# Two graph layers on one core: 36 batches of 31 sorted and 14 plain tiles, edge rows loaded whole in two parts, layer 1's half packed by ScalarE

## The reference

```
h  = max(layernorm(x), 0)                                   # layer 0, GIN
m  = relu(h[src] + e16 @ W_edge.T + b_edge)                 # per edge
a  = h + segment_sum(m, dst)                                # per node
x  = x + relu(batchnorm(a @ W1.T + b1)) @ W2.T + b2
h  = max(layernorm(x), 0)                                   # layer 1
y  = relu(concat(h[src], e64) @ M_W.T + M_b)                # per edge
x  = x + relu(concat(h, segment_sum(y, dst)) @ U_W.T + U_b)
```

## Time and profile before

| what | value |
|---|---|
| timed runs, median of 3 | 4224.73 us |
| profiled execution: span from first to last instruction | 2879.7 us |
| its own time beside the span | none given by the profile; the timed median less the span is 1345.0 us |
| PE busy | 2027.5 us, 70% of the span |
| POOL busy | 2097.2 us, 73% |
| DVE busy | 1529.9 us, 53% |
| ACT busy | 958.6 us, 33% |
| mean granted TensorE clock | 0.824 |
| HBM read, written | 296.20 MB, 268.18 MB |

### The profile page before, as it was taken

How to read it: one execution, slowest core, us unless ns; L and a number is a source line. 1 busy time by engine, 2 the same in 40 slices (tenths; PEclk the granted TensorE clock), 3 DMA queues, 4 the chain that set the end, 5 groups by cost and what they waited for, 6 DMA issues and landing times.

```text
span 2879.7 us, 74534 instructions
## 1 busy us (share of the span) xinstructions
PE 2027.5 (70%) x25733; PEld 1830.1 (64%) x25733; DVE 1529.9 (53%) x2605; ACT 958.6 (33%) x2153; POOL 2097.2 (73%) x2185
## 2 busy tenths in 40 slices
PE   4678777677775777767676676766768776778772
PEld 4567666666665766657565576656647666667662
DVE  6655445344443445444454444534568776777671
ACT  2433333333332333323333233333353332323230
POOL 5777777777777777777777777777537777777774
PEclk9987887878878888788888888887869888888885
DMA  8877766777668766677667776675639998989861
GB/s 269 237 194 214 219 198 174 195 219 207 196 174 207 227 194 190 183 212 224 191 182 190 219 210 197 175 198 133 150 110 266 233 211 215 220 213 225 208 160 46
DMA packets 707917, 567.80 MB, mean 197 GB/s; under 512 B 495308, under 2 KB 609216, under 8 KB 703224
## 3 DMA queue, kind: packets, MB, share of 16 engines
q1 hardware_dynamic: 628632, 403.50, 55.1%
q0 software_dynamic: 69440, 107.94, 12.5%
q10 hardware_dynamic: 9632, 53.14, 5.3%
HBM read 296.20 MB, written 268.18 MB: 196 GB/s over the span
## 4 chain that ended last, share of the span: by engine, by line
POOL 30%; PE 24%; DMA 16%; issue 14%; SPq 7%; DVE 5%; ACT 3%; POOLq 1%; DVEq 0%; ACTq 0%
POOL edge_store L753 15%; POOL gathered_rows L783 15%; PE ps_w L1228 10%; DMA src_store<-arena 8%; PE ps_p L1163 6%; SPq L564 5%; PE ps_r L1216 4%; DMA side<-attr 4%; DMA edge_store<-side,slot_idx 2%; ACT arena L926 1%; DMA gathered_rows<-node_table_l,plain_slot 1%; PE ps_b L1198 1%; SPq L491 1%; DMA arena<-edge_store 1%; DVE ranking L1524 1%
## 5 line engine op out<-in xcount | busy, mean ns | idle before, releaser
L783 POOL DMA_INDIRECT gathered_rows<-node_table_l,plain_slot x1116 | 1066.1, 955 | 359.3 <-issue 327.2
L753 POOL DMA_INDIRECT edge_store<-side,slot_idx x1054 | 1023.3, 971 | 344.8 <-issue 325.0
L1228 PE MATMUL ps_w<-arena 128*64 128x128 f32 (+1 forms) x9040 | 922.0, 293 | 204.5 <-ACT window L934 195.7
L1228 PEld LDWEIGHTS ps_w<-arena 128*64 128x64 f32 x9040 | 787.0, 158 | 264.7 <-ACT window L934 147.3
L939 ACT ACTIVATE arena<-arena 128x512 f32<-128x512 f32 (+1 forms) x616 | 366.3, 595 | 1533.1 <-PE ps_w L1228 925.9
L1163 PE MATMUL ps_p<-w_both,side 80*128 80x128 f32 x3228 | 519.6, 317 | 425.2 <-DMA side<-attr 344.1
L1163 PEld LDWEIGHTS ps_p<-w_both,side 80*128 80x128 f32 x3228 | 461.5, 223 | 446.4 <-issue 404.0
L1630 DVE TENSOR_TENSOR arena<-ps_c,dst_rel 128x1024 f32<-128x1024 f32 (+1 forms) x476 | 525.9, 1105 | 336.1 <-PE ps_w L1228 332.7
L1615 DVE TENSOR_SCALAR arena<-arena,iota_p 125x512 bf16<-125x512 bf16 (+1 forms) x442 | 155.9, 370 | 604.5 <-DMA src_store<-arena 371.6
L1216 PE MATMUL ps_r<-tab,arena 125*128 125x64 bf16 x5100 | 245.9, 202 | 102.5 <-DVE arena L1615 60.8
L1639 DVE TENSOR_TENSOR arena<-ps_r,arena 128x512 f32<-128x512 f32 (+1 forms) x476 | 297.6, 625 | 20.3 <-PE ps_r L1216 13.4
(11 more groups left out here) (124 smaller groups left out, 1057.4 us busy)
## 6 DMA issues: line engine op xcount, KB each, us to landing
edge_store<-zeros SPq DMA_DIRECT2D x34, 3300.0 KB
arena<-edge_store SPq DMA_DIRECT2D x34, 1650.0 KB, 10.7
src_store<-arena SPq DMA_DIRECT2D x204, 256.0 KB
side<-attr SPq DMA_DIRECT2D x172, 256.0 KB
arena<-edge_store SPq DMA_DIRECT2D x34, 1056.0 KB
arena<-edge_store SPq DMA_DIRECT2D x34, 594.0 KB
plain_store<-plain_e SPq DMA_DIRECT2D x35, 512.0 KB
side<-plain_store SPq DMA_DIRECT2D x35, 512.0 KB
```

The lines of the kernel that those rows point to most:

```text
L753: pool.indirect_dma_start(out=store, in_=stage[:, c, i, :], in_offset=None, out_offset=bass.IndirectOffsetOnAxis(ap=slot_idx[:, s, t + i:t ...
L783: pool.indirect_dma_start(out=rows[s][:, i, :], out_offset=None, in_=table[layer], in_offset=bass.IndirectOffsetOnAxis(ap=plain_slot[:, s, ...
L1228: mm = pe.matmul(ps_sum[layer][t % 2][:, 0:width], msg[:, slot, t, :], dst_match[:, slot, t, 0:width], start=(first and t <= layer), stop= ...
```

## The change

Batches become 31 sorted and 14 plain tiles, 36 of them (1620 tiles of room for 1612 used); groups and plain parts are equal in number, and the last plain part has 6 tiles. All loops end after 36 groups; one `last_plain` is left in each layer. The two plain units have 8 and 6 tiles.

In layer 0 a group's rows are loaded whole (528 bytes each, so that a partition's columns are one run): columns 0 to 23 (units 0 to 2) to a double buffer `early`, columns 24 to 49 (units 3 to 6) to a single buffer `late_rows`, which is loaded for the next group when the last unit of this group has been used and packed. ACT reads the marks of each part separately. After each relu of a sorted unit ACT copies the 66 floats with the marks and layer 1's half of each row to one of two slots of `halved` (`pack`) and stores them to a new table `edge_half` (`store_half`), whose rows are in the order of the reader. Layer 1 loads its part from there, in runs of 8448 and 4752 bytes a partition. `load_early` of group m+2 waits for unit 2 of group m used and packed. The core of the diff:

```diff
-PLAIN = 16
+PLAIN = 14
-TILES = 1645
-BATCHES = TILES // BATCH
-NB = BATCHES - 1
-PARTS = BATCHES
+NB = 36
+TILES = NB * BATCH
+BATCHES = NB
+PARTS = NB
+EARLY_UNITS = 3
+EARLY = EARLY_UNITS * UNIT
+LATE = NODE_COLS - EARLY
-PAIR_HALVES = (-1, 0, 1, 1, 2, 2, 3, 4)
+PAIR_HALVES = (-1, 0, 1, 1, 2, 3, 4)
-PAIR_UNITS = (0, 0, 1, 2, 3, 4, 5, 6)
+PAIR_UNITS = (0, 0, 1, 2, 3, 4, 5)
...
+    edge_half = nc.dram_tensor("edge_half", (NB, P, NODE_COLS * HALF_ROW), F32, kind="Internal").ap()
...
-            def load_edges(g, p):
-                sp.dma_start(edge[p], store_groups[bass.ds(g, 1), 0:CAP * NODE_COLS, 0:HALF_ROW]
-                             .rearrange("a (p j) c -> p (a j) c", j=NODE_COLS)).then_inc(dense_sems[0].e_landed[p], 16)
+            def load_early(g, p):
+                sp.dma_start(early[p].rearrange("p j c -> p (j c)"), store_groups[bass.ds(g, 1), 0:CAP * NODE_COLS, :]
+                             .rearrange("a (p j) c -> p (a j c)", j=NODE_COLS)[:, 0:early_cols]).then_inc(dense_sems[0].e_landed[p], 16)
+
+            def load_late(g):
+                sp.wait_ge(dense_sems[0].rows_used, units(g - 1, NU - 1) + 2)
+                sp.wait_ge(halves_packed, units(g - 1, NU - 1))
+                sp.dma_start(late_rows.rearrange("p j c -> p (j c)"), store_groups[bass.ds(g, 1), 0:CAP * NODE_COLS, :]
+                             .rearrange("a (p j) c -> p (a j c)", j=NODE_COLS)[:, early_cols:]).then_inc(dense_sems[0].late_landed, 16)
             def load_edges_part(g, p, k):
                 j, nj = LOAD_PARTS[k]
-                sp.dma_start(edge[p][:, j:j + nj, :], store_groups[bass.ds(g, 1), 0:CAP * NODE_COLS, D:D + HALF_ROW]
-                             .rearrange("a (p j) c -> p (a j) c", j=NODE_COLS)[:, j:j + nj, :]).then_inc(dense_sems[1].e_landed[p], 16)
+                sp.dma_start(edge[p][:, j:j + nj, :].rearrange("p j c -> p (j c)"),
+                             edge_half[bass.ds(g, 1), :, j * HALF_ROW:(j + nj) * HALF_ROW].rearrange("a p c -> (a p) c"))\
+                    .then_inc(dense_sems[1].e_landed[p], 16)
...
             def next_edges(m, s):
                 group_landed(m + 2)
-                sp.wait_ge(dense_sems[0].rows_used, units(m, NU - 1) + 2)
-                load_edges(m + 2, s)
+                sp.wait_ge(dense_sems[0].rows_used, units(m, EARLY_UNITS - 1) + 2)
+                sp.wait_ge(halves_packed, units(m, EARLY_UNITS - 1))
+                load_early(m + 2, s)
...
+                if not (isinstance(m, int) and m + 2 >= NB):
+                    load_late(m + 2)
                 for q in range(2):
                     load(m + 1, q if not isinstance(m, int) or m + 1 <= LAST_PREPARED else NQ + q)
                 store_plain(m)
...
+            def pack(g, gn, p, u):
+                slot, nt = (p + u) % 2, UNITS[u][1]
+                if not (isinstance(gn, int) and src_stores(gn, p, u) == 0):
+                    act.wait_ge(halves_stored[slot], src_stores(gn, p, u) * 16)
+                act.activation(halved[:, slot, 0:nt, :], edge_rows(p, u)[:, :, META:META + HALF_ROW], ACT.Copy).then_inc(halves_packed, 1)
+
+            def store_half(g, p, u):
+                slot, (j, nt) = (p + u) % 2, UNITS[u]
+                act.wait_ge(halves_packed, units(g, u))
+                act.dma_start(edge_half[bass.ds(g, 1), :, j * HALF_ROW:(j + nt) * HALF_ROW].rearrange("a p c -> (a p) c"),
+                              halved[:, slot, 0:nt, :].rearrange("p t c -> p (t c)")).then_inc(halves_stored[slot], 16)
...
                 for u, (j, nt) in enumerate(UNITS):
                     if layer == 0:
+                        if u == 1:
+                            read_late(m + 1, p)
                         for i in range(2 * u + 2, min(2 * u + 4, NH)):
                             copy_spread(m + 1, p, i)
                     act.wait_ge(d.rows_used, units(m + 1, u) + 2)
                     relu(layer, at + u, (par + u) % 2, nt)
+                    if layer == 0:
+                        pack(m + 1, n + s, p, u)
+                        if u:
+                            store_half(m + 1, p, u - 1)
...
+                if layer == 0:
+                    store_half(m + 1, p, NU - 1)
```

More of the change, by code:

```diff
@@ L220, in attr_loads, with metas @@
     return m * (NL // 2) + (FIRST_LOADS // 2 + q // 2 + 1)
+def metas(layer, g, k):
+    return g * 4 + 2 * (k + 1) if layer == 0 else g + 1
 def src_stores(bn, p, u):
@@ L420, in build @@
         src_matched = sem("src_matched")
+        halves_packed = sem("halves_packed")
+        halves_stored = [sem(f"halves_stored{s}") for s in range(2)]
         src_stored = [sem(f"src_stored{s}") for s in range(2)]
@@ L664, in turn @@
                         load(m, (2, 3, 4, 5).index(u) + 2)
-                    if u == 4:
+                    if u == 4 and not (isinstance(m, int) and m + 2 >= PARTS):
                         next_plain_idx(0, n, s)
@@ L679, in _ @@
                 turn(m // 2, m % 2, more=m <= LAST_PREPARED, more_fill=False)
-            for q in range(2):
-                load(PARTS - 1, NQ + q)
-            for m in range(NB - 1, PARTS):
-                store_plain(m)
+            store_plain(PARTS - 1)
             if_general(sp, general_flag(sp), lambda: general(0))
             sp.wait_ge(dense_sems[0].rows_used, NB * NU + 2)
+            for slot in range(2):
+                sp.wait_ge(halves_stored[slot], NB // 2 * NU * 16)
             for g in range(2):
@@ L723, in turn_l1 @@
                 m = n * 2 + s
-                next_plain_idx(1, n, s)
+                later = not (isinstance(m, int) and m + 2 >= PARTS)
+                if later:
+                    next_plain_idx(1, n, s)
                 if more:
                     next_group(m + 1, 1 - s)
-                next_plain(m, s)
+                if later:
+                    next_plain(m, s)
             next_group(0, 0)
@@ L826, in _ @@
             gather_plain(1, 0, 1)
-            with pool.Fori(1, NB // 2) as n:
+            with pool.Fori(1, NB // 2 - 1) as n:
                 for s in range(2):
                     gather_plain(1, n, s, paced=True)
-            gather_plain(1, NB // 2, 0)
+            for s in range(2):
+                gather_plain(1, NB // 2 - 1, s, paced=True)
             if_general(pool, general_flag(pool), lambda: general(1))
@@ L1073, in _ @@
             more = general_flag(act)
-            for m in range(NB - 1, PARTS):
-                last_plain(0, m)
+            last_plain(0, NB - 1)
             last_windows(0)
@@ L1110, in _ @@
             more = general_flag(act)
-            for m in range(NB - 1, PARTS):
-                last_plain(1, m)
+            last_plain(1, NB - 1)
             last_windows(1)
@@ L1633, in bucket_step @@
             def bucket_step(layer, g, p, u, step, slot):
[L1634 to L1636 removed]
+                d, (j, nt) = dense_sems[layer], UNITS[u]
+                if u == 0 or layer == 0 and u == EARLY_UNITS:
+                    dve.wait_ge(d.meta_done, metas(layer, g, 1 if u else 0))
                 dve.wait_ge(d.gathered, units(g, u))
@@ L1711, in last_windows @@
             def last_windows(layer):
-                for m in range(NB - 1, PARTS):
+                for m in range(NB - 2, NB):
                     accumulate(layer, NB + m, NB + m, PLAIN_WINDOW)
```

87 lines of the change are left out of this document (57 added, 30 removed).

## The result

Fourteen runs of each kernel on one chip: the changed kernel takes 4267.23 us (4249.62 to 4273.96), the kernel before 4224.4 us (4197.59 to 4247.52). The ratio is 1.010, with a 95% interval of 1.0079 to 1.0121. I had forecast 4180, faster. The time lies inside the range that I gave (4140 to 4280), the direction is wrong.

The account below looks back on a forecast made before the run. POOL (GpSimd), working nearly without a break, was taken as the bound. Layer 1 -78 and layer 0 +33 gave -45 us, so 4180 against the median 4224.73; the sum's own range was 4151 to 4210, the full range 4140 to 4280.

Parts of the forecast that it names:

- The step that failed: Outside the traced span: 1345.0 us between the profiled 2879.7 and the timed median 4224.73, unexplained, kept unchanged.
- Rival (c): Outside the span: the 1345.0 us stretch with it (4159, 8 in 100) or follow declared HBM memory (4654, 2 in 100).
- rival (a): Layer 0, at ACT's pack: dense work becomes the bound once packing adds over 4.4 us; 4270 us, 22 in 100.
- rival (d): Layer 1: period doesn't fall because PE at its lower clock becomes the bound; +42, 4267 us, 3 in 100.
- Layer 1: From its second batch, 542 POOL gathers become 482; -78 us, between -44 and -86.
- Steady turn: Layer 0: POOL's 14 gathers and 31 scatters make a turn 56.9 us, idle only in 0.3 us gaps.
- First turn: Layer 0: the single-buffered late rows load late and POOL waits for slots(); +5 us (0 to 12).
- Layer 0 to the statistics: Layer 0 ends at 2111.8, +33 us over 2078.45: 9 from steady and first turns, 24 from lost cover.
- the lost cover: End of layer 0: POOL has 34 gathers left instead of 62 to hide dense work; 24 us (12 to 36).
- Wait for the pack's stores: Layer 0: the pack waits for an earlier store; 2 us a turn, between 0 and 12, within the cover.
- Cover: Layer 0, steady turn: 52.5 us of dense work in 56.9, leaving 4.4 us to hide the packing's waits.
- DMA time of a turn: Layer 0: the engines' 42.7 us a turn grow by 8, to 51 of 56.9.

Follow-up runs that it names:

- r17: Changed kernel without the pack and its store, plus one semaphore increment ahead of each scatter matmul: 4232.31 us, 1.0102 of the plain kernel before, long condition.
- r1: The kernel before, unchanged, profiled once more: 2885.61 us, short condition.
- r3: The changed kernel, unchanged, beside the kernel before in the short condition: 2839.07 us, 0.9862 of the kernel before.
- r10: Changed kernel with each pack made three times (two more copies, a drain after each), short condition: 2976.18 us, 1.0347 of the kernel before.
- r4: Changed kernel without the pack and its store, layer 1 reading short pieces from edge_store, short condition: 2826.06 us, 0.9817 of the kernel before.
- r5: Kernel before with the matmuls of gathers and projections issued three times over, same result: 3573.99 us, 1.240 of the plain kernel before.
- r6: Changed kernel with the matmuls of gathers and projections issued three times over: 3623.81 us, 1.2582 of the plain kernel before.
- r12: Changed kernel with one semaphore increment ahead of each scatter matmul, long condition: 4257.5 us, 1.0179 of the plain kernel before.
- r18: Kernel before with one of each gather's three matmuls and an increment ahead of each scatter matmul, long condition: 4048.9 us, 0.9681 of the plain kernel before.
- r14: Kernel before with only one of the three matmuls of each gather, short condition: 1.0026 of the plain kernel before.
- r11: Kernel before with one semaphore increment ahead of each scatter matmul, long condition: 4176.18 us, 0.997 of the plain kernel before.

## Why the prediction was wrong, point by point

**The step that failed** is the first: "1345.0 us lie outside what the trace shows; no row says what they are ... and keep the 1345.0 us as they are". Nothing lies there. In every run that followed, span and time differ by some 2 us. The 1345.0 us stood between two conditions: the profile was of the short one, the timed runs of the long. In the long one the premise of all that follows, that a turn of layer 0 is all POOL, doesn't hold: a turn is 88.7 us, of which POOL works 57, and two turns more cost what PE and the engines behind it need for them (+114.6 us in layer 0), not the +33 of the sum. Rival (c) looked at this gap and asked only how it scales.

That the time lies in the range is luck, since the range was added up in the other condition. So is the nearness of rivals (a) and (d), 4270 and 4267: (a) laid it on the packing, and most of the loss stays without it (r17); (d) laid it on a layer 1 that gains nothing, and it gains 33.7 us.

**Within the condition that the trace shows** the working held. Forecast -45 us; measured -41.5 (timed), -47.6 (the spans of r1 and r3).
- Layer 1: -78, measured -78.5. Its second batch starts 81.5 us (r1) and 81.6 us (r3) after the statistics, as the prediction kept it.
- Steady turn: 56.9 us, measured 57.1, with 0.3 us gaps.
- First turn: +5 (0 to 12), measured 11.07 - 3.75 = +7.3.
- Layer 0 to the statistics: +33, measured +30.9. Less 7.3 and the steady +4 of the forecast, the lost cover is 19.6 of the 24 predicted (12 to 36).
- Wait for the pack's stores: 2 us a turn, measured 80.3 / 36 = 2.2, in range 0 to 12. The estimate of 2.6 us a store, from the Trainium skill (DMA: Bandwidth & Descriptors, "Anatomy of one DMA"), by which the pack would wait for nothing, doesn't agree with these 58 waits, the longest of 8.3 us. Its fit is one of DMAs that GpSimd issues, and this store is ScalarE's.
- Cover: 4.4 us was too little. Its terms, 50.3 - 1 + 3, give 52.3 and not 52.5; and while the 2 us of waits were still to come out of the 4.4, r10 found 5.4 to 8.8 us beyond them. So rival (a) was less near than priced, though it decides once 9 us more of packing are added.
- DMA time of a turn: 51 of 56.9 us; two turns of r3 have shares of 0.79 and 0.83, 45 to 47 us. The sum mixed two kinds of time: it took off 10.7 us, which is the time from issue to landing of the old load, and added 12.2 and 6.1 us of the engines' busy time. ACT's queue went from 5.5% of the span (r1) to 12.3% (r3), some 5.3 us a turn for the packed half, so the whole rows in long runs cost the engines about what the half rows in short pieces had. From issue to landing, 1584 KB in long runs took 7.2 us, 1650 KB in short pieces 10.7.
- Too low in the sum: what the packing adds at the end of layer 0. Without it (r4) the statistics start 18.9 us sooner; 9 of these lie in the first turn and 9.4 after the last turn's first gather, where the sum had 3. Other terms of the end came out lower, so that the total held by luck in part.
- The range of the sum, -15 to -74, isn't what its terms' ends give: added up they reach from +8 to -70.

**Why the sign turns.** Where POOL sets the pace the split is cheap in layer 0 (+30.9 us with the packing): it keeps its 1612 indirect transfers, and most of what two more turns cost comes back as shorter turns (59.7 to 57.1 us) and fewer gathers at the end. In the long condition a turn loses only 0.9 us of 88.8, two more turns cost nearly in full, and layer 1 gives back 33.7 us instead of 78.5. That more work on PE turns the sign is shown by r5 and r6. That PE's late issue does it in the long condition is read from the three parts of its span; no run changed it alone. That 4.4 us of cover said nothing of an engine 70% busy in the earlier trace rows was a lack: rival (d) named PE only for layer 1, and gave it 3 in 100.

**Left open.** What the long condition is. One chip was met in both, so it isn't the chip alone. Why r12 is at 1.018 where the changed kernel of the result is at 1.010: the increments, the chip or both. How much of the loss is the packing: PE's idle time without a wait is 658 us without it (r17) and 755 with it (r12), one trace each. And which wait comes forward in r18, since most of its semaphore records are missing.

No version that was measured in both conditions beats the kernel before in both. The changed kernel without packing is the best in the short one (0.9817 and 0.981), and 1.0102 in the long one. The split alone was never met in the long one.

## What to carry to other kernels

Before a sum is made in a trace, its span must agree with the time that is to be forecast: a gap of a third is a sign that the two are of different conditions, and then the question is which engine paces in the other one. A split that moves work off the pacing engine by adding turns is worth its gathers only while that engine paces; price the added turns by the whole turn of the next engine as well. Cover read from release to idle, as in the earlier trace rows, was an underestimate here (4.4 against at least 5.4 us); an experiment that adds work has to count drains and grown waits beside the busy time, or it confirms too much. And an engine's idle time before instructions that wait on nothing tells at once whether a trace is of a condition in which that engine is held up itself.

## What the runs showed that I had not expected

- Instructions that wait on nothing and still come late, in one condition only. In the trace of the result 453 matmuls follow the one before at 0.68 to 0.80 us; in r3, the same kernel, 14 do. SyncE shows it as well: of 3876 register and semaphore instructions 189 last over 250 ns there, 1 in r3. The instructions of DVE, ACT and POOL have the same median durations in both. The bytes of instructions fetched are equal in both (q8, the result's trace and then r3's), and tripling PE's work (r5) fetched 7.70 MB with 12 such steps, so it isn't their amount. Whether it is their fetch at all no run shows.

```profile
q8 instruction: 185, 3.03, 0.3%
```

```profile
q8 instruction: 186, 3.05, 0.5%
```

- With a third of the gather (r14) the same queue moves 0.64 MB instead of 2.95: 180 pieces of 16 KB become 39, so that most of the loops' code seems to be fetched once. The time hardly changes in the short condition. In the long one the kernel with a third of the gather also had the increments (r18) and fetched 160 pieces, so what fetching once would do there wasn't seen.

```profile
q8 instruction: 39, 0.64, 0.1%
```

- The result's trace holds 27683 semaphore events where r3's, of the same kernel, holds 63386. So many of its waits are put down to "remote" or "another core" in a kernel that runs on one core: such rows most likely mean that the releaser's record is missing; no other core runs. For the same reason an "issue" before an instruction that does wait may hide a wait.
- The mean granted clock (between its levels of 1.2 and 2.4 GHz) differs with the condition: 0.69 in the result and 0.70 in r11, with PE busy 65% and 66% of the span; 0.82 in r1 with 71%, and 0.95 in r5 with 90%. The busy share alone doesn't tell it: r14, busy 66% in the short condition, was granted 0.79. The scatter's matmuls took 327 ns a piece in the result and 293 in r3, the same kernel.
